# Placing the softmax rows of a transformer layer: a broadcast copy and a second transfer, or a short copy and one transfer

## The chip, the cores and the metric

The kernel runs on one core of a Trainium2 chip, as one launch. The metric is the device time of a run in microseconds. The kernel before took 1909.01, 1910.10 and 1910.19 us in three runs, with a median of 1910.1 us. The profiled execution is the first of them.

## The reference

A transformer block with 16 sequences of 256 positions and 512 features: self attention, cross attention to a context of 256 positions, and a feed-forward part of 2048 hidden features, each behind a layer norm whose gain and offset come from a conditioning vector.

```python
def _attn(q, k, v):                                   # 16 heads of 32 features
    scores = jnp.einsum('bqhd,bkhd->bhqk', q, k) * scale
    w = jax.nn.softmax(scores, axis=-1)
    return jnp.einsum('bhqk,bkhd->bqhd', w, v).reshape(B, L, D)

x = x + _attn(rope(xn1 @ Wq), rope(xn1 @ Wk), xn1 @ Wv) @ Wo        # xn1 = adaln(x, emb, ln1)
x = x + _attn(rope(xn2 @ Wq2), rope(ctx @ Wk2), ctx @ Wv2) @ Wo2    # xn2 = adaln(x, emb, ln2)
x = x + gelu(xn3 @ W1.T + b1) @ W2.T + b2                           # xn3 = adaln(x, emb, ln3)
```

## The kernel before

Every float32 product is made of three products of split operands (high by high, high by low, low by high). The kernel has two parts. The first, up to some 1210 us, does both attention layers: 32 items (16 sequences in each of two layers), each with 16 heads, so 512 heads in a row, in one order that all engines follow. The second part is the feed-forward, which the change does not touch.

The order is written out by `stage_order(B)`. It loops over the heads n and gives each head three places, 3n, 3n+1 and 3n+2. Place 3n begins with the score product of head n ("scores", line 619 on TensorE, the row maximum on VectorE at line 865, and exp with a row sum on ScalarE at line 750, step "total", at place 3n+2). Place 3n+1 begins with the second, transposed score product of head n-13 ("weigh", line 640; `LAG = 13`), whose exp on ScalarE (line 764) writes the probabilities that the "mix" step (line 655) takes. Projections, rotations, norms and loads are put at places between. Each engine has its own function (`attention_tensor`, `attention_scalar`, `attention_vector`, `attention_gpsimd`, `attention_sync`) that walks the same order and does its part of each step in that order, with semaphore waits; so a step that waits holds up all that stands behind it on its engine.

The change is about how the softmax shift enters the "weigh" product. Heads are handled in groups G of eight (64 groups; two per item; groups 0 to 31 are the first layer). For each group VectorE forms minus the row maximum minus the log of the row sum, split into a high and a low part: 16 numbers for each query ("max_split", lines 873 to 878, `max_parts`). TensorE transposes them ("max_turn", line 626), and they become rows 96 to 111 of `qT`, the moving operand of "weigh", below 96 rows of head data. `kT`, the stationary one, holds in its rows 96 to 111 a table of ones and zeros (`select`, written once by six ScalarE copies at the start) that picks, for each head, its high and its low row. `max_parts` is 112 columns wide with 96 columns of zeros, so that the transposed rows come out at partitions 96 to 111. There ScalarE copies them into `qT`, repeated four times for the four heads of a quad ("max_copy", line 732, 16 partitions by 1024 elements, semaphore `rows_placed`). A transfer from the SyncE queue copies the same rows to the second quad of the group ("max_again", line 1004, semaphore `rows_again`). The first weigh of a group waits for `rows_placed`, its fifth for `rows_again`.

The score-side results go through five PSUM banks in turn (`score_users`, `NS = 5`): "scores", "weigh", "max_turn" and "mix" each take the next bank, and TensorE waits (`scores_left`) until the user five before has been read.

## Time and profile before

| what | value |
|---|---|
| median of three runs | 1910.1 us |
| the profiled execution, its span | 1909.01 us, 1907.2 us |
| TensorE matmul busy | 1869.2 us, 98% |
| ScalarE, VectorE, GpSimd busy | 1434.9, 1289.4, 787.3 us |
| mean granted clock | 0.996 |
| line 732, the broadcast copies | 64, 65.3 us in all |
| line 1004, the second transfers | 64 of 64 KB, 3.0 us from issue to landing (median) |

The span is the time from the first to the last instruction; the run's time has some 1.8 us around it. A matmul's end is modelled in the profile, so TensorE at 98% can still hold short pauses; they show as gaps between the starts. PE is TensorE's matmul, PEld its weight load, ACT ScalarE, DVE VectorE, POOL GpSimd, and a q behind a name (SPq, ACTq) marks an instruction that the engine's sequencer runs, such as the issue of a transfer.

### The profile page before, as it was taken

How to read it: one execution, taken by the hardware profiler on the slowest of the kernel's cores; microseconds unless marked ns; L12 is line 12 of the kernel's file. 1: busy time of each engine (PE TensorE's matmuls, PEld its weight loads, DVE VectorE, ACT ScalarE, POOL GpSimd, SP SyncE). 2: the span in 40 equal slices, each digit the busy share in tenths (PEclk: the TensorE clock that was granted, in tenths of full speed). 3: DMA queues.
4: the chain of work that ended last, by engine and by line, in shares of the span. 5: the costliest groups of instructions: out<-in, count | busy, mean ns of one | idle time of the engine just before them, and what ended most of it. 6: DMA issues, size and time to landing. Idle time of an engine off the chain costs nothing. (4 is left out here: it accounts for less than half of the span.)

```text
span 1907.2 us, 39347 instructions
## 1 busy us (share of the span) xinstructions
PE 1869.2 (98%) x13460; PEld 1632.0 (86%) x13460; DVE 1289.4 (68%) x2249; ACT 1434.9 (75%) x3819; POOL 787.3 (41%) x818
## 2 busy tenths in 40 slices
PE   8899999999998999999999998999999999999999
PEld 6888888888887988988988987688898998989898
DVE  6877667777766776776776777346766667666754
ACT  5888888888887898888888899655656566666654
POOL 3634334433433454454454441014535445453531
PEclk9999999999998999999999999999999999999999
DMA  7777767676686787677677687433131322323130
GB/s 230 206 210 211 219 196 202 195 209 179 194 233 179 210 237 224 190 223 215 194 222 219 192 230 196 130 111 117 61 111 56 111 78 89 100 70 109 45 100 34
DMA packets 307378, 311.51 MB, mean 163 GB/s; under 512 B 22000, under 2 KB 259952, under 8 KB 307184
## 3 DMA queue, kind: packets, MB, share of 16 engines
q1 hardware_dynamic: 306576, 308.67, 55.4%
q8 instruction: 111, 1.82, 0.4%
q14 instruction: 83, 0.68, 0.1%
q10 hardware_dynamic: 608, 0.34, 0.1%
HBM read 212.46 MB, written 92.27 MB: 160 GB/s over the span
## 5 line engine op out<-in xcount | busy, mean ns | idle before, releaser
L750 ACT ACTIVATE ps_s<-ps_s,neg_max 128x256 f32<-128x256 f32 x1024 | 461.6, 454 | 45.4 <-DVE neg_max L865 42.3
L865 DVE TENSOR_REDUCE neg_max<-ps_s 128x2 f32<-128x512 f32 x512 | 349.7, 687 | 210.1 <-PE ps_s L619 209.6
L764 ACT ACTIVATE prob<-ps_s 128x512 f32<-128x512 f32 x512 | 307.9, 602 | 98.7 <-PE ps_s L640 94.4
L619 PE MATMUL ps_s<-kT,qT 96*128 96x256 f32 x1024 | 218.6, 295 | 11.7 <-ACT ps_s L750 7.5
L935 POOL TENSOR_TENSOR rope_c<-rope_c,rope_s 128x256 f32<-128x256 f32 x128 | 98.6, 771 | 312.9 <-DVE rope_s L840 312.9
L619 PEld LDWEIGHTS ps_s<-kT,qT 96*128 96x128 f32 x1024 | 168.7, 190 | 59.5 <-ACT ps_s L750 24.5
L640 PE MATMUL ps_s<-qT,kT 112*128 112x256 f32 x1024 | 208.2, 285 | 9.9 <-ACT ps_s L750 9.3
L750 ACT ACTIVATION_READ_ACCUMULATOR ps_s<-ps_s,neg_max 128x1 f32 x1024 | 217.9, 213 | 0.0
L609 PE MATMUL ps_g<-xx_hi,w_hi 128*128 128x256 f32 x1024 | 208.0, 284 | 1.4 <-issue 1.4
L609 PE MATMUL ps_g<-xx_hi,w_lo 128*128 128x256 f32 x1024 | 205.6, 282 | 0.0
L609 PE MATMUL ps_g<-xx_lo,w_hi 128*128 128x256 f32 x1024 | 205.4, 282 | 0.0
L1306 PE MATMUL ps_y<-w_hi,h_hi 128*128 128x512 f32 x512 | 201.5, 394 | 1.2 <-DVE h_lo L1431 1.2
L1306 PE MATMUL ps_y<-w_lo,h_hi 128*128 128x512 f32 x512 | 200.6, 392 | 0.0
L1306 PE MATMUL ps_y<-w_hi,h_lo 128*128 128x512 f32 x512 | 199.3, 389 | 0.0
L640 PEld LDWEIGHTS ps_s<-qT,kT 112*128 112x128 f32 x1024 | 169.5, 190 | 31.3 <-ACT ps_s L750 12.1
L1431 DVE TENSOR_TENSOR h_lo<-h_sb,h_hi 128x512 fp32r<-128x512 f32 x128 | 111.5, 875 | 103.9 <-ACT h_hi L1329 102.6
L942 POOL TENSOR_TENSOR rot_lo<-rope_c,rot_hi 128x512 fp32r<-128x512 f32 x128 | 166.1, 1298 | 30.4 <-ACT rot_hi L726 28.6
L923 POOL TENSOR_TENSOR xx_lo<-xT,xx_hi 128x512 fp32r<-128x512 f32 x66 | 86.9, 1318 | 197.0 <-ACT xx_hi L712 196.8
L1290 PE MATMUL ps_h<-xf_hi,cw_hi 128*128 128x256 f32 x592 | 167.5, 283 | 0.0
L1290 PE MATMUL ps_h<-xf_lo,cw_hi 128*128 128x256 f32 x592 | 165.8, 280 | 0.0
L1290 PE MATMUL ps_h<-xf_hi,cw_lo 128*128 128x256 f32 x592 | 165.7, 280 | 0.0
L609 PEld LDWEIGHTS ps_g<-xx_hi,w_hi 128*128 128x128 f32 x1024 | 158.2, 190 | 2.6 <-issue 1.5
(155 smaller groups left out, 4708.4 us busy)
## 6 DMA issues: line engine op xcount, KB each, us to landing
kT<-k_turned SPq DMA_DIRECT2D x384, 128.0 KB, 3.2
qT<-q_turned SPq DMA_DIRECT2D x128, 256.0 KB, 4.0
f_raw<-in_w1T SPq DMA_DIRECT2D x124, 256.0 KB, 3.0
k_turned<-rot_hi SPq DMA_DIRECT2D x64, 256.0 KB, 3.2
k_turned<-rot_lo SPq DMA_DIRECT2D x64, 256.0 KB, 2.5
q_turned<-rot_hi SPq DMA_DIRECT2D x64, 256.0 KB, 3.8
q_turned<-rot_lo SPq DMA_DIRECT2D x64, 256.0 KB, 4.2
qT<-q_turned SPq DMA_DIRECT2D x128, 128.0 KB, 4.1
```

Of the source, the lines that this page charges most:

```text
L609: ins = eng.matmul(ps_g[:, b, s * L:(s + 1) * L], w[:, row, (T * s + t) * P:(T * s + t + 1) * P], a[:, c, :], start=c == 0 and j == 0 and ...
L619: ins = eng.matmul(ps_s[:, score_bank(step), t * L:(t + 1) * L], qT[0:ROWS, quad % NQ, j, t * P:(t + 1) * P], kT[0:ROWS, quad % NQ, j, :], ...
L640: ins = eng.matmul(ps_s[:, score_bank(step), t * L:(t + 1) * L], kT[:, quad % NQ, j, t * P:(t + 1) * P], qT[:, quad % NQ, j, :], start=Tru ...
L750: ins = eng.activation(scores[:, t * L:(t + 1) * L], scores[:, t * L:(t + 1) * L], ACT.Exp, bias=neg_max[G % 2][:, t, j:j + 1], accum_out= ...
L764: eng.activation(prob[:, n % NP, :, :].rearrange("p t l -> p (t l)"), ps_s[:, score_bank(step), :], ACT.Exp).then_inc(exp_done, 1)
L865: eng.tensor_reduce(neg_max[G % 2][:, :, j], ps_s[:, score_bank(step), :].rearrange("p (t l) -> p t l", l=L), AX.X, ALU.max, negate=True). ...
L923: eng.tensor_tensor(lo[:, ks, :], xT[:, ks, :], hi[:, ks, :].bitcast(F32), ALU.subtract).then_inc(x_low_done, 1)
L935: eng.tensor_tensor(rope_c[n % 2][:, 0, :], rope_c[n % 2][:, 0, :], rope_s[:, 0, :], ALU.subtract)
L942: eng.tensor_tensor(rot_lo[:, n % NT, :, :], rope_c[n % 2][:, :, :], rot_hi[:, n % NT, :, :].bitcast(F32), ALU.subtract).then_inc(rot_lo_d ...
L1290: ins = eng.matmul(ps_h[:, bank(p, n), 0:L], w[:, cols], x_[:, k, :], start=n in OPENS and k == 0 and j == 0, stop=k == 1 and j == 2, skip ...
L1306: ins = eng.matmul(ps_y[:, t, :], h[:, t * P:(t + 1) * P], w, start=c == 0 and j == 0, stop=c == FC - 1 and j == 2)
L1431: eng.tensor_tensor(h_lo[a % NH][:, :], h_sb[a % 2][:, :], h_hi[a % NH][:, :].bitcast(F32), ALU.subtract).then_inc(h_lo_done, 1)
```

## The change

The group's 16 rows are laid out as 2 partitions by 8 heads instead of 16 partitions repeated for 4 heads, so that one high and one low row stand in `qT` below each head's own data, and `kT` needs only ones there. The operand has 98 rows instead of 112. Per group: the transposes yield 16 rows; ScalarE copies 16 partitions by 256 elements into a staging buffer `max_rows`; and one transfer issued from ScalarE's queue ("max_rows") puts them into both quads. The transfer from SyncE's queue is gone, and the first weigh of a group now waits for the landing of the transfer (`max_rows_in`). The "max_turn" step stays at place 32 of the group in the first layer and moves to place 30 in the second; the copy follows one place later and the transfer two places later. The six copies of `select` on ScalarE and its load are gone; a memset on VectorE writes the ones near the start.

```diff
-        for n, kind in ((24, "log"), (25, "max_split"), (32, "max_turn"), (33, "max_copy"), (35, "max_again")):
+        turn = 32 if G < 2 * B else 30
+        for n, kind in ((24, "log"), (25, "max_split"), (turn, "max_turn"), (turn + 1, "max_copy"), (turn + 2, "max_rows")):
             put(24 * G + n, kind, G)
...
     yield ("warm", WARM_START)
+    yield ("ones",)
...
-    for slot in range(2):
-        yield ("select", slot)                        # and twice more, six in all
...
-    MROWS = ROWS + 2 * HG
+    MROWS = ROWS + 2
...
-            max_parts = sb("max_parts", [P, T, MROWS])
-            select = sb("select", [P, HG])
+            max_parts = sb("max_parts", [P, T, ROWS])
+            max_rows = [sb(f"max_rows{n}", [2 * HG, L], F32R) for n in range(2)]
...
-                return {"scores": total_done, "weigh": exp_done, "max_turn": rows_placed, "mix": o_lo_done}[old[0]], nth[old]
+                return {"scores": total_done, "weigh": exp_done, "max_turn": maxes_copied, "mix": o_lo_done}[old[0]], nth[old]
...
-                            ins = eng.transpose(ps_s[0:MROWS, score_bank(step), t * P:(t + 1) * P],
-                                                max_parts[:, t, :], ident[:, :])
+                            ins = eng.transpose(ps_s[0:2 * HG, score_bank(step), t * P:(t + 1) * P],
+                                                max_parts[:, t, 0:2 * HG], ident[:, :])
...
                         if n % HG == 0:
                             G = n // HG
-                            eng.wait_ge(rows_placed, G + 1)
-                        elif n % HG == OH:
-                            eng.wait_ge(rows_again[n // HG % 2], 16 * (n // HG // 2 + 1))
+                            eng.wait_ge(max_rows_in[G % 2], 16 * (G // 2 + 1))
...
                     elif kind == "max_copy":
                         G = step[1]
                         eng.wait_ge(max_turned, G + 1)
+                        if G >= 2:
+                            eng.wait_ge(max_rows_in[G % 2], 16 * (G // 2))
+                        eng.activation(max_rows[G % 2][:, :], ps_s[0:2 * HG, score_bank(("max_turn", G)), 0:L],
+                                       ACT.Copy).then_inc(maxes_copied, 1)
+                    elif kind == "max_rows":
+                        G = step[1]
+                        eng.wait_ge(maxes_copied, G + 1)
                         if G >= NQ // 2:
                             eng.wait_ge(weigh_done, HG * (G - NQ // 2 + 1))
-                        eng.activation(qT[ROWS:MROWS, 2 * G % NQ, :, :],
-                                       ps_s[ROWS:MROWS, score_bank(("max_turn", G)), 0:L].unsqueeze(1).broadcast_to([2 * HG, OH, L]),
-                                       ACT.Copy).then_inc(rows_placed, 1)
+                        first = 2 * G % NQ
+                        into = qT[ROWS:MROWS, first:first + 2, :, :]
+                        eng.dma_start(into.rearrange("p g h l -> p (g h) l").bitcast(F32),
+                                      max_rows[G % 2][:, :].bitcast(F32)).then_inc(max_rows_in[G % 2], 16)
...
+                    elif kind == "ones":
+                        eng.memset(kT[ROWS:MROWS, :, :, :].bitcast(F32), 1.0).then_inc(ones_set, 1)
...
-                    elif kind == "max_again":
-                        G = step[1]
-                        eng.wait_ge(rows_placed, G + 1)
-                        eng.dma_start(qT[ROWS:MROWS, (2 * G + 1) % NQ, :, :].bitcast(F32),
-                                      qT[ROWS:MROWS, 2 * G % NQ, :, :].bitcast(F32)).then_inc(rows_again[G % 2], 16)
```

How the instructions move, at two places. First ScalarE around the copy of group 13 (odd, first layer): "total" rows are the exp with sum, `prob` rows the exp of weigh, `rot_hi` a rotated half. Before:

```order
L750 ACTIVATE ps_s,total<-ps_s,neg_max 128x256 x2
L764 ACTIVATE prob<-ps_s 128x512
L750 ACTIVATE ps_s,total<-ps_s,neg_max 128x256 x2
L732 ACTIVATE qT<-ps_s 16x1024
L764 ACTIVATE prob<-ps_s 128x512
L726 ACTIVATE rot_hi<-rope_c 128x512
L750 ACTIVATE ps_s,total<-ps_s,neg_max 128x256 x2
L764 ACTIVATE prob<-ps_s 128x512
```

and the same place now:

```order
L744 ACTIVATE ps_s,total<-ps_s,neg_max 128x256 x2
L758 ACTIVATE prob<-ps_s 128x512
L744 ACTIVATE ps_s,total<-ps_s,neg_max 128x256 x2
L725 ACTIVATE max_rows<-ps_s 16x256
L758 ACTIVATE prob<-ps_s 128x512
L719 ACTIVATE rot_hi<-rope_c 128x512
L734 DMA qT<-max_rows 2x8x256
L744 ACTIVATE ps_s,total<-ps_s,neg_max 128x256 x2
L758 ACTIVATE prob<-ps_s 128x512
```

The copy keeps its place and is shorter; the transfer stands behind an exp and a rotation. In the even groups of the first layer it stands behind the exp alone. Second, ScalarE around the copy of group 40 (even, second layer). Before:

```order
L764 ACTIVATE prob<-ps_s 128x512
L750 ACTIVATE ps_s,total<-ps_s,neg_max 128x256 x2
L726 ACTIVATE rot_hi<-rope_c 128x512
L732 ACTIVATE qT<-ps_s 16x1024
L764 ACTIVATE prob<-ps_s 128x512
L750 ACTIVATE ps_s,total<-ps_s,neg_max 128x256 x2
```

and the same place now:

```order
L758 ACTIVATE prob<-ps_s 128x512
L725 ACTIVATE max_rows<-ps_s 16x256
L744 ACTIVATE ps_s,total<-ps_s,neg_max 128x256 x2
L719 ACTIVATE rot_hi<-rope_c 128x512
L734 DMA qT<-max_rows 2x8x256
L758 ACTIVATE prob<-ps_s 128x512
```

The copy has moved ahead of a pair of exps with sum, and the transfer takes the place of the old copy. In the odd groups of the second layer no rotation stands between.

## Rows read from the trace of the kernel before

**Rows 1.** Busy time by stretch: us, then each engine's busy us (instructions), clock, DMA.
```profile
100.00:550.00 450.00, 448.02 (x3553) 386.02 (x3552) 322.19 (x587) 377.58 (x1133) 177.75 (x186) 1.00 0.70 201
584.00:594.50 10.50, 7.05 (x43) 4.06 (x44) 5.06 (x8) 9.49 (x27) 4.38 (x4) 0.51 0.77 209
600.00:1125.00 525.00, 524.25 (x4156) 460.13 (x4155) 366.80 (x693) 457.33 (x1368) 243.61 (x248) 1.00 0.73 211
1125.00:1207.00 82.00, 73.89 (x572) 59.90 (x571) 55.31 (x111) 77.28 (x237) 18.93 (x19) 1.00 0.65 174
```

**Rows 2.** Groups: line engine op, shapes, count | busy us, mean ns | idle before, releasers.
```profile
L732 ACT ACTIVATE qT<-ps_s 16x1024 fp32r<-16x1024 f32 x64 | 65.3, 1020 | 1.9 <-PE ps_s L626 0.3
L1334 ACT ACTIVATE u_sb<-ps_h 128x256 f32<-128x256 f32 x168 | 64.4, 383 | 83.1 <-PE ps_h L1290 81.9
L619 PE MATMUL ps_s<-kT,qT 96*128 96x256 f32 x1024 | 218.6, 295 | 11.7 <-ACT ps_s L750 7.5 <-ACT qT L732 1.5 <-DMA qT<-q_turned 1.5
L640 PE MATMUL ps_s<-qT,kT 112*128 112x256 f32 x1024 | 208.2, 285 | 9.9 <-ACT ps_s L750 9.3 <-DVE o_lo L884 0.6
L626 PE MATMUL ps_s<-ident,max_parts 128*112 128x128 f32 x128 | 24.4, 272 | 0.0
L582 PE MATMUL ps_g<-ident,xn 128*128 128x128 f32 x272 | 40.8, 273 | 1.3 <-DVE rope_s L840 1.3
```

**Rows 3.** Timeline, all engines, group 13: start us, us, engine line operation.
```profile
304.01 1.02 ACT L732 ACTIVATE qT<-ps_s 16x1024 fp32r<-16x1024 f32 x1
...
304.91 0.54 SPq L1000 DMA_DIRECT2D q_turned<-rot_lo  x1
...
305.06 0.60 ACT L764 ACTIVATE prob<-ps_s 128x512 f32<-128x512 f32 x1
...
305.55 0.62 ACT L726 ACTIVATE rot_hi<-rope_c 128x512 fp32r<-128x512 f32 x1
...
307.22 0.31 PEld L640 LDWEIGHTS ps_s<-qT,kT 112*128 112x128 f32 x2
307.33 0.40 PE L640 MATMUL ps_s<-qT,kT 112*128 112x256 f32 x2
```

**Rows 4.** Line 1000, stretch 304 to 307: its one transfer's landing.
```profile
DMA to landing us min/median/max: 2.4/2.4/2.4
```

**Rows 5.** Line 1004, whole span: landing of its 64 transfers.
```profile
DMA to landing us min/median/max: 2.3/3.0/6.2
```

**Rows 6.** Timeline around the copy of group 16, first layer.
```profile
359.44 1.02 ACT L732 ACTIVATE qT<-ps_s 16x1024 fp32r<-16x1024 f32 x1
360.49 0.60 ACT L764 ACTIVATE prob<-ps_s 128x512 f32<-128x512 f32 x1
...
362.57 0.31 PEld L640 LDWEIGHTS ps_s<-qT,kT 112*128 112x128 f32 x2
```

**Rows 7.** Timeline around the copy of group 40, second layer.
```profile
807.82 0.60 ACT L764 ACTIVATE prob<-ps_s 128x512 f32<-128x512 f32 x1 [0.38 <-PE ps_s L640]
...
809.22 0.64 ACT L726 ACTIVATE rot_hi<-rope_c 128x512 fp32r<-128x512 f32 x1
...
812.51 0.31 PEld L640 LDWEIGHTS ps_s<-qT,kT 112*128 112x128 f32 x2
```

**Rows 8.** Line 1004, stretch 560 to 595 (groups 27 and 28): landing.
```profile
DMA to landing us min/median/max: 4.9/5.3/5.7
```

**Rows 9.** Timeline at 563 us: a weigh that waited.
```profile
563.73 0.50 PE L640 MATMUL ps_s<-qT,kT 112*128 112x256 f32 x2 [1.43 <-ACT ps_s L750]
```

**Rows 10.** Lines 740 and 777: durations min/median/max ns; first statistics on VectorE.
```profile
L740 ACT ACTIVATE kT<-select x6: 1032/1046/1057, 27.9 to 37.4; 16x1024 fp32r<-16x1024 f32 x6
...
L777 DVE MEMSET max_parts<- x1: 245/245/245, 0.9 to 0.9; 128x224 f32 x1
...
8.67 0.69 DVE L787 BATCH_NORM_STATS2 stats<-xn 128x6 f32<-128x512 f32 x1 [7.53 <-DMA xn<-in_x]
```

**Rows 11.** Page, part 3: the SyncE queue's packets, MB, share of 16 engines.
```profile
q1 hardware_dynamic: 306576, 308.67, 55.4%
```

More of the change, by code:

```diff
@@ L217, in stage_order @@
     yield from rotated("q", 0)
-    for slot in range(2, 4):
-        yield ("select", slot)
     yield ("stack", "k", 0)
@@ L225, in stage_order @@
     yield from rotated("k", 1)
-    for slot in range(4, 6):
-        yield ("select", slot)
     for c in range(2, KC):
@@ L419, in block_kernel @@
             mod_parts = [prob_row[:, 2 * KC * D:(2 * KC + 1) * D], w_raw[:, 0, :], w_raw[:, 0, :]]
-            small_in = {name: sem(f"{name}_in") for name in ("cond", "lnb", "ident", "cos", "sin", "select")}
+            small_in = {name: sem(f"{name}_in") for name in ("cond", "lnb", "ident", "cos", "sin")}
             x_in, res_in, ctx_in = (sem(n) for n in ("x_in", "res_in", "ctx_in"))
@@ L424, in block_kernel @@
             stack_in = {m: [sem(f"stack_{m}{n}") for n in range(4)] for m in "qk"}
-            rows_placed, rows_again = sem("rows_placed"), [sem(f"rows_again{n}") for n in range(2)]
+            max_rows_in = [sem(f"max_rows_in{n}") for n in range(2)]
             STACKS = {"q": 2, "k": 3}
@@ L433, in block_kernel @@
             mod_copied = sem("mod_copied")
-            w_hi_done, x_full, x_hi_done, ctx_hi_done, rot_hi_done, v_done, exp_done, total_done, log_done, o_hi_done = (
+            w_hi_done, x_full, x_hi_done, ctx_hi_done, rot_hi_done, v_done, maxes_copied, exp_done, total_done, log_done, o_hi_done = (
                 sem(n) for n in ("w_hi_done", "x_full", "x_hi_done", "ctx_hi_done", "rot_hi_done", "v_done",
-                                 "exp_done", "total_done", "log_done", "o_hi_done"))
+                                 "maxes_copied", "exp_done", "total_done", "log_done", "o_hi_done"))
             parts_cleared = sem("parts_cleared")
@@ L440, in block_kernel @@
             early_done, early_kept = sem("early_done"), sem("early_kept")
-            constants_set, select_set, mod_summed, mod_added, norm_stats, norm_means, norm_var, x_normed, x_low_done, ctx_low_done = (
-                sem(n) for n in ("constants_set", "select_set", "mod_summed", "mod_added", "norm_stats", "norm_means", "norm_var",
+            constants_set, ones_set, mod_summed, mod_added, norm_stats, norm_means, norm_var, x_normed, x_low_done, ctx_low_done = (
+                sem(n) for n in ("constants_set", "ones_set", "mod_summed", "mod_added", "norm_stats", "norm_means", "norm_var",
                                  "x_normed", "x_low_done", "ctx_low_done"))
@@ L662, in attention_scalar @@
                 eng.dma_start(ident[:, :], ident_in).then_inc(small_in["ident"], 16)
-                eng.dma_start(select[ROWS:MROWS, :], pick).then_inc(small_in["select"], 16)
                 eng.dma_start(ln_b[:, :, :], lnb).then_inc(small_in["lnb"], 16)
@@ L729, in attention_scalar @@
                         eng.wait_ge(max_turned, G + 1)
+                        if G >= 2:
[5 more added lines that the diff above has]
+                        eng.wait_ge(maxes_copied, G + 1)
                         if G >= NQ // 2:
                             eng.wait_ge(weigh_done, HG * (G - NQ // 2 + 1))
-                        eng.activation(qT[ROWS:MROWS, 2 * G % NQ, :, :],
-                                       ps_s[ROWS:MROWS, score_bank(("max_turn", G)), 0:L].unsqueeze(1).broadcast_to([2 * HG, OH, L]),
-                                       ACT.Copy).then_inc(rows_placed, 1)
-                    elif kind == "select":
-                        slot = step[1]
-                        if slot == 0:
-                            eng.wait_ge(small_in["select"], 16)
-                        first = slot % 2 * OH
-                        eng.activation(kT[ROWS:MROWS, slot, :, :], select[ROWS:MROWS, first:first + OH].unsqueeze(2).broadcast_to([2 * HG, OH, L]),
-                                       ACT.Copy).then_inc(select_set, 1)
+                        first = 2 * G % NQ
+                        into = qT[ROWS:MROWS, first:first + 2, :, :]
+                        eng.dma_start(into.rearrange("p g h l -> p (g h) l").bitcast(F32),
+                                      max_rows[G % 2][:, :].bitcast(F32)).then_inc(max_rows_in[G % 2], 16)
                     elif kind == "total":
@@ L776, in attention_vector @@
             def attention_vector(eng):
-                eng.memset(max_parts[:, :, :], 0.0).then_inc(parts_cleared, 1)
+                eng.memset(max_parts[:, :, 0:ROWS], 0.0).then_inc(parts_cleared, 1)
                 eng.memset(neg_half[:, :], -0.5).then_inc(constants_set, 1)
```

6 lines of the change are left out of this document (3 added, 3 removed).

## The prediction

> **What bounds the kernel now.** I read the busy times by stretch first. In the steady part of both attention layers TensorE is busy 448.02 of 450 us and 524.25 of 525 us, at the full granted clock of 1.00, while ScalarE, the next, is busy 84% and 87% [rows 1]. So the reader should see a TensorE that hardly ever waits there: time taken off ScalarE gives nothing back in these 975 us, and any new wait of TensorE is paid in full. Only the last stretch of the second layer, 1125 to 1207 us, is different: TensorE 73.89 of 82 us, ScalarE 77.28 of 82, which is 94% [rows 1]. Of the weigh products' waits over the whole span, 9.3 us were for the exps of line 750 [rows 2]. Smaller stretches of that kind are the first groups and the change of layer, where a piece of 10.5 us ran at a granted clock of 0.51, TensorE's lower level (1.2 GHz) [rows 1]. Over the whole span the two score products stood idle 11.7 and 9.9 us [rows 2]; that is about all that a lighter ScalarE could ever buy.
>
> **The copy.** It shrinks from 1020 ns to about 383 ns, the mean of another ScalarE copy of 256 elements out of PSUM [rows 2]. That is 0.64 us for each of 64 groups, 41 us of ScalarE's time. In the steady part TensorE covers all of it: value 0. In the ScalarE-bound stretch there are six groups (58 to 63), so at most 6 x 0.64 = 3.8 us. But ScalarE's queue also gets the transfer's issue, which holds a sequencer for 0.54 us [rows 3]. If it lies beside a running exp it costs nothing, if not it eats nearly the whole gain: between 0 and 3.8 us, and I take a gain of 1.5, since in these groups the issue stands behind the short read of the row sum, which can't cover it.
>
> **The transfer in front of weigh.** This is the term that matters. Before, the first weigh waited for a ScalarE copy that was long done. Now it waits for a chain: copy, the exp behind it, in odd groups a rotation too, issue, landing. Queued behind a waiting weigh on TensorE is everything, and all other engines live off that.
>
> Odd groups of the first layer. The copy starts at 304.01 and would end at 304.39; the exp, which followed the old copy by 0.03 us, starts at 304.42. The rotation followed that exp by 0.49 us, so 304.91; it had not waited for its input. The issue comes with it, about 304.95. The weight load of the first weigh stood at 307.22 [rows 3]: 2.27 us are left. A transfer that SyncE issued at 304.91, the same moment, took 2.4 us to land [rows 4]; the old row transfers never took less than 2.3 [rows 5]. I take 2.4 to 2.5: it lands at 307.4, 0.2 us late. A product that had to wait also starts worse, as a pair takes 0.50 us instead of 0.40 [rows 3, 9], so 0.3 us a group. There are 14 such groups (3 to 29): 4.2 us.
>
> Even groups of the first layer. The tighter kind, group 16 and eight others like it: copy 359.44 to 359.82, exp at 359.85, issue at 359.90; the weight load is at 362.57, so 2.67 us are left [rows 6], more than 2.5. Cost 0, but with 0.2 us to spare. The rest have some 0.4 us more.
>
> Second layer. The copy now follows the exp at 807.82 by 0.50 us: 808.32 to 808.70, then the pair of exps with sum (0.90 us, from 808.32 to the rotation at 809.22), the rotation at 809.63, the issue at 809.67, and 2.84 us are left until 812.51 [rows 7]. Cost 0. The odd groups have no rotation in between and more room. The exps with sum finish 0.4 us later than before there; the bank they free is needed only by the score product of two heads later, so this is covered.
>
> Groups 0, 1, 27 and 28 stand where the DMA engines are crowded. The row transfers there took 4.9 to 5.7 us [rows 8], against 2.3 to 2.8 us of room: 2 us or more late each at worst, nothing at best if the transfer, now alone in its own queue, overtakes. As ScalarE bounds there and has work in stock while TensorE waits, part is hidden. I take 2 us in all (0 to 8).
>
> **The rest.** Weigh has 98 rows instead of 112: 96-row and 112-row products took 295 and 285 ns, so fewer rows buy nothing [rows 2]; 0. The transposes of 112 and of 128 columns took 272 and 273 ns [rows 2], so 16 columns change nothing I can see; 0, at most 128 x 0.03 = 4 us if a short weight load counts for once. The six select copies (6 x 1.046 us) lie between 27.9 and 38.5 us [rows 10], where ScalarE otherwise waits for rotations; 0.1 us gained. The memset of 2 x 6144 elements, at 245 ns for 224 elements, is 6.7 us and ends at 7.8; VectorE's next work began at 8.67, when its input had landed [rows 10]. Covered by that load; uncovered it would cost up to 6.7. SyncE loses 64 issues of some 0.6 us and their waits, and nothing there is late in the steady part: 0.
>
> **Sum.** 4.2 + 2.0 - 1.5 - 0.1 = +4.6 us on the profiled execution's 1909.01 us, which is 1913.6. That execution lies 1.1 us below the median of its three runs, so I forecast 1914 us, against 1910.1. What a measurement of this kernel can tell from no change is 0.2%, or 3.8 us, so this lies on the edge.
>
> **Rival 1, eight rows in a line (slower).** The target is only two partitions. If the 16 KB don't spread over all DMA engines but go as eight 1 KB packets one behind the other, each of 55 ns (0.554 x 16 x 1907.2 us / 306576 packets) [rows 11], landing comes 0.4 us later, and 0.8 if each alternates with SyncE's. With a landing of 2.8: odd groups 0.53 + 0.1 late, x 14 = 8.8; nine tight even groups 0.13 + 0.1, 2.1; second layer 0. With 2.5 for the rest, 1920 to 1922. With 3.3 it reaches 16 + 7 + 1, plus the second layer's even groups at 0.56 x 13 = 7, 1940. It decides once landing exceeds about 2.7 us.
> The Trainium skill has a rule that speaks for this rival: "DMA: Bandwidth & Descriptors", section "Why a DMA increments its semaphore by 16 and not by 1", says that a hardware-issued transfer is spread over the largest number up to 16 that divides the slowest dimension on both sides, which for 2 rows of target is two engines. No row of before shows which engines a transfer used. By that rule the sum would be some 1921, by the row of line 1000 alone 1914.
>
> **Rival 2, ScalarE's time comes back (faster).** Ten groups lie where ScalarE bounds: 10 x 0.64 = 6.4 us if the issues are hidden beside exps, and if TensorE's pause before 584 us shrinks, the piece at half clock goes too, worth up to half of its 10.5 us, 5. That needs rows that land in time: 1898 to 1903. For it speaks the 94% [rows 1], against it that all waits of the two score products come to 21.6 us, first stretches included [rows 2], and that the transfer adds its own latency.
>
> **Rival 3, all hidden.** Landing takes 2.3 us and the crowded groups overtake: 1908 to 1911.
>
> **Chances.** Forecast 0.35, rival 1 0.20, rival 2 0.20, rival 3 0.25. All of rival 2 is faster: 0.20. No change is rival 3 and a third of the forecast: 0.37. Slower is the rest, 0.43. The range leaves out the low end of rival 2 and the far end of rival 1: 1902 to 1925; the forecast's own is 1910 to 1919.
>
> **What would show it.** Right: weigh (640 before) waits for "DMA qT<-max_rows" in some 14 groups of the first layer, 0.1 to 0.3 us each, and none in the second; the new transfer lands in 2.4 to 2.5 us; ScalarE some 41 us less busy; the stretch 1125 to 1207 about 1.5 us shorter. Wrong: waits for that transfer in even groups as well, or a landing over 2.7 us (rival 1); no wait at all (rival 3); a granted clock that stays at 1.00 near 584 us (rival 2); VectorE's first statistics after 8.7 us.

## The result, and the profile after

The changed kernel took 1929.57 us (median of four runs, 1926.05 to 1929.88) against 1910.14 for the kernel before; the ratio is 1.0095, with an interval of 1.0078 to 1.0112. It is slower, and outside the predicted range of 1902 to 1925. The profiled execution took 1925.28 us, with a span of 1923.5 us; that is 16.3 us more than the 1909.01 us of before.

Busy time by stretch in the changed kernel, with the columns of [rows 1]; the last row is a second of the places where TensorE ran at its lower level:

```profile
100.00:550.00 450.00, 440.63 (x3461) 377.72 (x3460) 314.76 (x572) 354.74 (x1110) 172.86 (x180) 1.00 0.66 196
600.00:1125.00 525.00, 521.50 (x4119) 456.65 (x4120) 366.80 (x692) 435.89 (x1372) 244.04 (x248) 0.99 0.72 210
577.80:581.20 3.40, 3.40 (x31) 1.66 (x24) 0.21 (x1) 2.44 (x7) 0.00 (x0) 0.51 1.04 340
```

Against [rows 1] TensorE has lost 7.4 us of work in the 450 us of the first layer, and ScalarE has 22.8 us less to do there. Most of the loss is in the first layer and at its ends; the rest is in the last groups. The groups of the page and of the view by line that answer to [rows 2]:

```profile
L725 ACT ACTIVATE max_rows<-ps_s 16x256 fp32r<-16x256 f32 x64 | 22.8, 357 | 0.0
L615 PE MATMUL ps_s<-kT,qT 96*128 96x256 f32 x1024 | 216.5, 293 | 10.7 <-ACT ps_s L744 8.3 <-DVE o_lo L880 1.0 <-DMA qT<-q_turned 0.7
L634 PE MATMUL ps_s<-qT,kT 98*128 98x256 f32 x1024 | 211.6, 289 | 24.4 <-DMA qT<-max_rows 21.8 <-ACT ps_s L744 1.9 <-DVE o_lo L880 0.6
L622 PE MATMUL ps_s<-ident,max_parts 128*16 128x128 f32 x128 | 24.4, 271 | 2.2 <-ACT ps_s L744 2.2
L622 PEld LDWEIGHTS ps_s<-ident,max_parts 128*16 128x16 f32 x128 | 11.0, 88 | 6.9 <-ACT ps_s L744 2.8 <-ACT prob L758 0.3
```

Weigh (line 634 now) waits 21.8 us for the new transfer, where [rows 2] has no such entry at all. The waits, by group, from TensorE's idle time before the first weigh: none in any odd group from 3 to 29; in the even groups 2, 6, 8, 12, 18, 20 and 26 of the first layer 2.4, 1.8, 1.2, 1.1, 0.6, 0.2 and 1.5 us (8.9 together, where the expectation of number 1 below has 9.1); in groups 1, 27, 28, 30, 59, 60 and 62 1.7, 2.3, 2.8, 0.4, 1.3, 4.0 and 0.5 us (13.0 together).

The semaphores' events in the trace give the landing of each of the 64 transfers: 2.2 us at the least, 2.29 in the median, 6.2 at the most. Each transfer raises its semaphore three times, about 1.1 us after the issue and twice at the end. In a quiet group its sixteen 1 KB packets go in pairs, eight steps in 0.45 us; in group 6 they go as two runs of eight, one starting 0.5 us behind the other.

Group 13, the place of [rows 3]; timeline of ScalarE's engine and queue, start us, us, engine line operation:

```profile
313.63 0.36 ACT L725 ACTIVATE max_rows<-ps_s 16x256 fp32r<-16x256 f32 x1
...
313.90 0.57 ACT L758 ACTIVATE prob<-ps_s 128x512 f32<-128x512 f32 x1
...
314.02 0.62 ACTq L734 DMA_DIRECT2D qT<-max_rows  x1
...
314.38 0.62 ACT L719 ACTIVATE rot_hi<-rope_c 128x512 fp32r<-128x512 f32 x1
```

The issue starts 0.03 us after the copy's end (313.99), while the exp runs, and ahead of the rotation that stands in front of it in the order. The weight load of the group's first weigh stands at 316.91 and its product at 317.02: there are 2.9 us of room, not 2.27, and the landing takes 2.25. In the even groups of the first layer the issue does not come so early: in group 16 the exp in front of it waits 0.37 us for its weigh product, and the issue starts 0.44 us after the copy's end, with 2.47 us left until the weight load.

Now two even groups of the first layer, 6 and 16, with the same order on ScalarE: first the timeline from the residual load of SyncE to the first weigh, then the stretches of 1 us from the issue on (last two columns: DMA share, GB/s).

```profile
175.82 0.43 SPq L1022 DMA_DIRECT2D res<-in_x  x1
...
176.30 0.47 SPq L968 DMA_DIRECT2D w_raw<-in_lnT  x1
...
178.04 0.65 ACTq L734 DMA_DIRECT2D qT<-max_rows  x1
...
182.58 0.47 PE L634 MATMUL ps_s<-qT,kT 98*128 98x256 f32 x2 [1.80 <-DMA qT<-max_rows]
```

```profile
366.97 0.43 SPq L1022 DMA_DIRECT2D res<-in_x  x1
...
369.66 0.62 ACTq L734 DMA_DIRECT2D qT<-max_rows  x1
...
372.24 0.40 PE L634 MATMUL ps_s<-qT,kT 98*128 98x256 f32 x2
```

```profile
178.04:179.04 1.00, 1.00 (x11) 1.00 (x10) 1.00 (x3) 0.84 (x2) 0.00 (x0) 1.00 1.12 243
179.04:180.04 1.00, 1.00 (x11) 1.00 (x10) 1.00 (x2) 1.00 (x5) 0.87 (x2) 1.00 1.03 324
180.04:181.04 1.00, 0.74 (x7) 0.54 (x5) 0.40 (x2) 0.98 (x4) 0.57 (x1) 1.00 1.10 397
...
369.66:370.66 1.00, 1.00 (x11) 1.00 (x10) 1.00 (x3) 0.87 (x2) 0.00 (x0) 1.00 0.98 348
370.66:371.66 1.00, 1.00 (x11) 1.00 (x10) 1.00 (x2) 1.00 (x5) 0.87 (x2) 1.00 0.15 45
```

In group 16 the DMA engines run empty 1 us after the issue; the first packet of the rows starts 1.27 us after it and they land in 2.24. In group 6 the engines are full for 3 us; the first packet starts after 3.0 us, the landing takes 4.41, and TensorE stands still for 1.80 us. In these two groups the 16 KB are in time only where SyncE's earlier transfers, 512 KB of residual above all, have drained.

Why does the residual load stand there at all? In the kernel before SyncE waited for the copy of the rows, to issue the second transfer, and the residual load stood behind that. Group 16 before, timeline of SyncE (the copy is the one of [rows 6], at 359.44):

```profile
360.50 0.57 SPq L1004 DMA_DIRECT2D qT<-qT  x1
361.11 0.58 SPq L1031 DMA_DIRECT2D res<-in_x  x1
```

The load came 1.67 us after the copy's start. The change took SyncE's wait away, and now the load is issued 2.69 us ahead of the rows (366.97 and 369.66 above). The same happened in group 60, where TensorE waits longest:

```profile
1174.52 0.43 SPq L1022 DMA_DIRECT2D res<-x_after_self  x1
```

The rows of group 60 are issued at 1175.77, 1.25 us behind it, and land after 6.2 us; the row transfer of before was issued there 0.63 us ahead of the residual load and landed in 2.35. So the 21.8 us of waits are of two kinds. In groups 6, 18, 20, 26 and 60, together 8.1 us, the old row transfer had landed in 2.3 to 2.4 us, and the load that came forward makes the new one late. In groups 1, 2, 8, 12, 27, 28, 30 and 59, together 13.2 us, the old one had already taken 3.0 to 6.2 us, unseen since its user came half a group later. Group 62 waits 0.5 us with a landing of 2.26: its place is too near.

**The sum.** Against the profile of before: waits for the rows +21.8; weigh's waits for the exps with sum from 9.3 to 1.9, so -7.4; the scores' idle time from 11.7 to 10.7, -1.0; the transposes' 0 to 2.2, +2.2; three pieces of 3.4 us at a granted clock of 0.50 that begin near the end of long waits (106.7, 577.7 and 1181.9 us) and that before did not have, half of 10.2, +5.1; and the transposes' weight load, 88 ns for 16 columns against 132 for 112, 128 x 0.044, -5.6. That is +15.1 of the 16.3. The waits are read off; the clock's term is an estimate, half of the time spent at the lower level; that the shorter load pays is argued, from its size and from the second layer: from group 32 to 57, without waits, the changed kernel gains 0.1 us a group on the one before.

### The profile page after: what moved, and what is told of

The parts are those of the page before. It is cut to its first block and busy times, and to the rows that moved or that the text cites. A ratio compares the mean times of both kernels' runs of the same rounds, so it can differ in the third digit from the quotient of the medians.

```text
span 1923.5 us, 39339 instructions
## 1 busy us (share of the span) xinstructions
PE 1869.4 (97%) x13460; PEld 1630.4 (85%) x13460; DVE 1294.9 (67%) x2250; ACT 1383.3 (72%) x3813; POOL 785.8 (41%) x818
## 5 line engine op out<-in xcount | busy, mean ns | idle before, releaser
L744 ACT ACTIVATE ps_s<-ps_s,neg_max 128x256 f32<-128x256 f32 x1024 | 452.8, 443 | 55.4 <-DVE neg_max L861 48.3
L758 ACT ACTIVATE prob<-ps_s 128x512 f32<-128x512 f32 x512 | 303.4, 593 | 137.2 <-PE ps_s L634 134.3
L634 PE MATMUL ps_s<-qT,kT 98*128 98x256 f32 x1024 | 211.6, 289 | 24.4 <-DMA qT<-max_rows 21.8
L615 PE MATMUL ps_s<-kT,qT 96*128 96x256 f32 x1024 | 216.5, 293 | 10.7 <-ACT ps_s L744 8.3
L634 PEld LDWEIGHTS ps_s<-qT,kT 98*128 98x128 f32 x1024 | 169.3, 191 | 46.9 <-issue 21.0
L744 ACT ACTIVATION_READ_ACCUMULATOR ps_s<-ps_s,neg_max 128x1 f32 x1024 | 207.8, 203 | 0.0
```

The costliest lines, as they stand in the source:

```text
L615: ins = eng.matmul(ps_s[:, score_bank(step), t * L:(t + 1) * L], qT[0:ROWS, quad % NQ, j, t * P:(t + 1) * P], kT[0:ROWS, quad % NQ, j, :], ...
L634: ins = eng.matmul(ps_s[:, score_bank(step), t * L:(t + 1) * L], kT[:, quad % NQ, j, t * P:(t + 1) * P], qT[:, quad % NQ, j, :], start=Tru ...
L744: ins = eng.activation(scores[:, t * L:(t + 1) * L], scores[:, t * L:(t + 1) * L], ACT.Exp, bias=neg_max[G % 2][:, t, j:j + 1], accum_out= ...
L758: eng.activation(prob[:, n % NP, :, :].rearrange("p t l -> p (t l)"), ps_s[:, score_bank(step), :], ACT.Exp).then_inc(exp_done, 1)
```

## The experiments

Twelve kernels, in three sittings; each ratio is to the kernel before, run on the same chip beside it. Unless said otherwise the edit is made to the changed kernel. Theory A is the latency: room of 2.6 to 3.0 us, and a landing that is 2.24 us plus whatever SyncE has put in front.

**1. The residual load seven places later.**

```diff
-            put(p + 37, "res_load", i - 1)
+            put(p + 44, "res_load", i - 1)
```

> The change, with one number altered: the step that loads the residual (512 KB on SyncE's queue) stands at place 44 of an item instead of 37, so behind the rows' transfer and its landing. Theory (collision): in the kernel before SyncE's queue itself waited for the row copy (line 1004) and so held the residual load back; now it is issued up to 2.7 us before the rows' transfer and fills the DMA engines while that is to land. Then the waits of weigh for the rows in the even groups of the first layer (9.1 us in the changed kernel) fall to 3 us or less, and the time falls by 5 to 9 us against the change, to about 1921 to 1924. Rival (few rings): the transfer is slow because its target is two partitions; then it lands late as before and the time stays at 1929. Groups 1, 27, 28, 59 and 60 are crowded for other reasons and stay.

Measured: 1933.92 us, ratio 1.0134 (1.0097 to 1.0170); waits for the rows 22.2 us, 16 times. A miss: I had expected 5 to 9 us less than the changed kernel, and it is no faster. The even groups 16 to 26 now landed in 2.23 to 2.29 us and did not wait, as A says, but groups 2, 6, 8, 10 and 12 still did, and the load now met the rows of odd groups 11, 15, 19, 25 and 31. The collision was moved, not removed.

**2. SyncE held back until the copy is done.**

```diff
+ (35, "hold"): on SyncE, eng.wait_ge(maxes_copied, G + 1)
```

> The change, and SyncE's queue waits at place 35 of each group until ScalarE has made the copy, as in the kernel before, but issues nothing there. Theory (collision): nothing that stands behind place 35 can be ahead of the rows' transfer any more; residual, weight and context loads and the stacks behind it come after. Waits for the rows fall from 21.8 us to 8 to 12 us (what is left is groups 1, 27, 28, 59 and 60, where the crowd is issued before the copy), and the time by 7 to 12 us against the change, to 1918 to 1922. Rival (few rings): no change, 1929.

Measured: 1942.17 us, ratio 1.0164 (1.0138 to 1.0190); waits 33.8 us, 19 times: a miss in sign. All even groups from 2 to 26 waited. Group 16, timeline:

```profile
379.16 0.40 SPq L1024 DMA_DIRECT2D res<-in_x  x1
...
379.57 0.62 ACTq L734 DMA_DIRECT2D qT<-max_rows  x1
```

SyncE is released by the same copy and issues its 512 KB 0.41 us ahead of ScalarE; the rows' first packet then starts 2.62 us after the issue in place of 1.27 (2.6 to 3.1 in groups 16 to 24), and they land after 3.89 us. To hold the other queue until the copy isn't enough: the load must stand behind the rows.

**3. The transposes at place 30 in both layers.**

```diff
-        turn = 32 if G < 2 * B else 30
+        turn = 30
```

> The change, with the transposes of a group at place 30 in the first layer too (32 in the change). This gives the chain copy, transfer, weigh two places more, some 1.5 us. Theory (collision): the late landings of 0.3 to 1.8 us in the first layer's even groups are covered but for the longest; waits fall by 6 to 9 us in the first layer, time about 1920 to 1923. The transposes may now wait for the split of the maxima, at most 0.5 us in a few groups. Rival (the latency isn't what costs, but ScalarE's queue with the issue in it): the time stays at 1929.

Measured: 1916.53 us, ratio 1.0027 (1.0016 to 1.0039). 13 us came back by nothing but room. Weigh and transposes:

```profile
L634 PE MATMUL ps_s<-qT,kT 98*128 98x256 f32 x1024 | 213.8, 291 | 13.3 <-DMA qT<-max_rows 9.5 <-ACT ps_s L744 3.2 <-DVE o_lo L880 0.6
L622 PE MATMUL ps_s<-ident,max_parts 128*16 128x128 f32 x128 | 24.4, 271 | 9.4 <-DVE max_parts L874 6.8 <-ACT ps_s L744 2.6
```

The waits for the rows fell from 21.8 to 9.5 us, though the landings in even groups did not get shorter (2.3 to 5.4 us). Of the new waits of the transposes for VectorE's split, 0.5 us in each of 14 odd groups, little reaches the time: over those groups the distance to the kernel before grows by 0.1 us each.

**4. The kernel before, its second transfer issued from ScalarE's queue.**

```diff
-  "max_again" in attention_sync
+  "max_again" in attention_scalar, same place
```

> The kernel before, with one part moved: the second transfer (qT to qT, line 1004) is issued from ScalarE's queue at the same place 35, so SyncE's queue no longer waits for the copy. Theory (collision): the residual load goes out earlier here too and the second transfer lands later in the even groups, but the fifth weigh has some 9 us for it, so nothing waits: within 0.1% of the kernel before, 1909 to 1912. Rival (freeing SyncE's queue disturbs the rest, for instance the stacks): slower by 3 us or more. Rival (an issue in ScalarE's queue costs 0.5 us each): slower in the stretch that ScalarE bounds, by up to 3 us.

Measured: 1910.74 us, ratio 0.9998 (0.9988 to 1.0007). Issues on ScalarE and a freer SyncE cost nothing where the transfer has half a group of slack.

But the landings change, and nothing else was moved in this kernel. Group 60, landing of the second transfer, first in the kernel before (line 1004, stretch 1163 to 1165), then here (line 738, stretch 1165.3 to 1165.5):

```profile
DMA to landing us min/median/max: 2.3/2.3/2.3
DMA to landing us min/median/max: 8.9/8.9/8.9
```

In groups 6, 18, 20 and 26 the landing was 2.3 to 2.4 us and is now 5.5, 4.0, 2.6 and 4.6; in groups 14, 16 and 22, where the residual load goes out 3.1 to 4.3 us ahead, it stays at 2.3. The residual load is now issued ahead of the transfer (in group 60 at 1162.70, the transfer at 1165.39). So it is the freed SyncE queue that makes these groups late, whatever the rows' layout; the change put a transfer that TensorE waits for into that place.

**5. A small residual load.** From the second sequence of the first layer on, the load brings 8 of 128 partitions.

```diff
-                        eng.dma_start(res[:, :, :], ...
+                        few = P if layer or i == 0 else 8
+                        eng.dma_start(res[0:few, :, :], ...
```

> In the first layer the residual load of SyncE (line 1022, 512 KB) brings only 8 of 128 partitions (32 KB), from the second batch on; the residual of those batches is therefore wrong, all else is the changed kernel. Nothing else moves. Theory A (the rows of maxima are late in even groups because the residual load, issued 2.2 to 2.7 us ahead from the other queue, is in front of them on the DMA engines): the waits of weigh in groups 6, 8, 12, 18, 20, 24, 26 (8.4 us together) go to under 1 us, group 2 (whose load stays whole) keeps its 2.5 us, as do 27, 28, 59, 60; sum of weigh's waits for max_rows 21.8 to about 13.5 us, time about 1921 us (1918 to 1924) against 1929.6 for the changed kernel. Rival (a transfer into two partitions on a queue of its own is slow now and then, whatever SyncE loads): waits stay near 22 us and the time near 1929.

Measured: 1924.59 us, ratio 1.0060 (1.0045 to 1.0074). Half a hit. In the even groups 14 to 24 every transfer landed in 2.24 to 2.46 us and none waited; group 18 went from 0.6 us to 0, group 20 from 0.2 to 0, group 26 from 1.5 to 0.4. That is 2 us of waits; in all the profiled execution, at 1933.70 us the slowest of the four, still waited 21.5 us for rows, 12 times, where I had expected 13.5. Groups 6, 8, 10 and 12 waited 1.5, 1.3, 1.8 and 1.7 us, together more than in the changed kernel, and groups 2, 28 and 59 3.2, 4.6 and 2.6. In groups 6 to 12 the rows' issue follows 1.6 to 2.7 us behind weight loads of 256 KB and, in 8, 10 and 12, 0.6 to 1.3 us behind a stack of `kT`, which the theory should have counted: what is in front is all of SyncE's queue, and the residual is the largest piece only from group 14 on.

**6. Rows of even groups from SyncE, ahead of the residual load; odd ones from ScalarE.**

```diff
 attention_scalar, "max_rows":   + if G % 2 == 0: continue
 attention_sync,   "max_rows":   + the same step, if G % 2: continue
```

> The rows of maxima of even groups are issued by SyncE at the place where the row transfer of before stood, directly ahead of the residual load; those of odd groups stay on ScalarE. Theory A (what counts is who stands in front on the DMA engines: in SyncE's own queue the residual load is generated after the rows): even groups 2 to 26 land in 2.3 to 2.6 us and wait no more than in before (0 to 1 us in all), left are groups 1, 27, 28, 59, 60 with perhaps 8 us; time 1917 us (1912 to 1922). Rival (what counts is the chain copy, issue, landing by itself): SyncE adds a wait for the copy and the issue comes no earlier, so even groups stay late: 1928 or more. A third way: the wait for the copy holds back SyncE's stack loads, and the products wait for kT or qT instead, which would show as a wait for k_turned or q_turned.

Measured: 1997.56 us, ratio 1.0448 (1.0430 to 1.0466): 80 us off my number, and both halves of it teach. The waits for the rows make 69.2 us, 24 times, and the very first weigh stands still for 6.4 us more. Group 16, timeline, and the wait of group 8 behind it:

```profile
388.63 0.36 ACT L725 ACTIVATE max_rows<-ps_s 16x256 fp32r<-16x256 f32 x1
...
389.02 0.68 SPq L1008 DMA_DIRECT2D qT<-max_rows  x1
...
389.74 0.40 SPq L1035 DMA_DIRECT2D res<-in_x  x1
...
392.01 0.40 PE L634 MATMUL ps_s<-qT,kT 98*128 98x256 f32 x2
```

```profile
220.20 0.36 ACT L725 ACTIVATE max_rows<-ps_s 16x256 fp32r<-16x256 f32 x1
...
222.76 0.60 SPq L1022 DMA_DIRECT2D qT<-q_turned  x1
223.41 0.43 SPq L970 DMA_DIRECT2D w_raw<-in_lnT  x1
223.93 0.70 SPq L1008 DMA_DIRECT2D qT<-max_rows  x1
...
228.15 0.47 PE L634 MATMUL ps_s<-qT,kT 98*128 98x256 f32 x2 [3.98 <-DMA qT<-max_rows]
```

Where SyncE is already waiting for the copy (groups 4, 6 and 14 to 26) the rows are issued 0.02 to 0.03 us behind it and land in 2.29 to 2.30 us (group 6: 2.85), with 512 KB right behind them; not one of these groups waits. This is what A says of the order in the queue. Where SyncE is still busy with what stands ahead in its own program (groups 8, 10, 12, and the even ones from 28 to 58) the issue comes 2.8 to 4.6 us after the copy's end, and weigh waits 2.0 to 9.0 us. The third way that I had named, waits for `qT` or `kT` in their place, hardly came (2.0 us, once).

**7. One head more between scores and weigh.**

```diff
-LAG = 13
+LAG = 14
```

> The changed kernel with weigh (and mix) following the scores by 14 heads instead of 13: one head more, some 2.27 us, lies between the copy and the first weigh of a group. Theory A (a latency that varies from 2.2 to 6 us against 2.6 to 3.0 us of room): with 4.9 to 5.3 us of room only groups 60 and perhaps 59 still wait, 1 to 2 us together; the extra half clock pieces go; the one head more costs about 1 to 2 us once at the end of the weighing; time 1913 us (1909 to 1918). Rival (the loss is TensorE's own: the transposes, the products of 98 rows or the clock): the time stays near 1929. Second rival (later weighing keeps the tiles of rotated q longer and makes SyncE's stack loads late): waits for q_turned in their place.

Measured: 1925.20 us, ratio 1.0063 (1.0050 to 1.0075); the profiled span is 1918.8.

```profile
PE ps_s L615 <- ACT ps_s L744: 10.9, 23, 2.1
PE ps_s L634 <- ACT ps_s L744: 5.8, 9, 1.6
PE ps_s L634 <- DMA qT<-max_rows: 3.6, 4, 1.7
```

(The columns are the us in total, the times, the longest.) The time is a miss, 12 us above my number; the waits for the rows are not far off, 3.6 us in 4 groups where I had expected 1 to 2, with landings of up to 6.9 us: they are hidden by room. The price was under-estimated: the other order lets the scores and weigh wait for ScalarE (10.9 and 5.8 us, against 8.3 and 1.9), and the distance to the kernel before grows by some 0.2 us a group in the first layer, where the changed kernel's fell by 0.1 between its waits. The sum of waits predicts the profiled span, not all of the median.

**8. The kernel before, transposes at 30 in its second layer.**

```diff
-        for n, kind in (..., (32, "max_turn"), (33, "max_copy"), (35, "max_again")):
+        turn = 32 if G < 2 * B else 30
+        for n, kind in (..., (turn, "max_turn"), (turn + 1, "max_copy"), (35, "max_again")):
```

> The kernel before, with only the other edit of the change's order: in the second layer the transposes and the copy of the maxima stand two places earlier (30 and 31 in place of 32 and 33), the copy still to all four heads. If the fall of 0.1 us a group that the changed kernel showed in its second layer comes from this move, the second layer gets 2.5 to 3 us shorter: 1907.5 us; if it comes from the lighter work of ScalarE or the 98 rows, the time is that of before within 1 us. I expect no change: 1910 (1908 to 1912).

Measured: 1923.75 us, ratio 1.0057 (1.0045 to 1.0069). A miss: not the same but slower.

```profile
PE ps_s L620 <- ACT ps_s L751: 16.2, 34, 2.2
```

(Us in total, times, the longest.) The scores wait 16.2 us for ScalarE against 7.5 before [rows 2], some 0.5 us in every second group from 38 on. Not all of it is the edit's: 3.6 us of the distance stand before the second layer, where nothing was moved, 6.5 us come between groups 37 and 59, and most of the rest behind them. With the long copy the earlier place doesn't fit; with the short one (the changed kernel) it costs nothing. So ScalarE's relief has a value after all: it pays for the move that the transfer needs (as number 11 shows).

**9. The place by parity.**

```diff
+        turn = 28 if G in (28, 60) else 32 if G < 2 * B and G % 2 else 30
```

> The changed kernel with max_turn at place 30 in even groups of the first layer (room to the first weigh 4.1 us in place of 2.6) and at 32 in odd ones (3.0 us, and no wait of the transposes for the split of VectorE, which cost 0.5 us in each odd group with 30 everywhere), and at 28 in groups 28 and 60. Theory A, summed from the run with 30 everywhere (1916.5): minus 14 x 0.5 for the transposes, minus about 2 for groups 28 and 60: 1908 us (1905 to 1913), with waits for max_rows of 6 us or less. Rival (what is gained in rows is paid again by the scores, whose bank ScalarE frees later, as in the kernel before with turn 30): 1915 or more.

Measured: 1923.41 us, ratio 1.0054 (1.0039 to 1.0068); waits for rows 14.7 us, 10 times. My sum was wrong by 15 us. Up to group 28 the run is level with number 3 (10.6 and 10.8 us behind before), so the 7 us that I had taken for the transposes' waits were not there to be had. The rest is lost between groups 28 and 29 (+4.3, where number 3 gains 1.4), beside the place 28; group 60's landing was 6.6 us and made nothing of its head start.

**10. The same with the residual load at 44.** The two edits of 9 and 1 together.

> The same with the residual load seven places later (44). Theory A: with even groups' rows now 1.5 us earlier, the later load is clear of them altogether, but it meets the odd groups' rows, which have only 3.0 us, as it did in the first run of this study (groups 11, 15, 19, 25, 31): no better than the run beside it, 1911 us (1906 to 1918). Rival (the load's place does not matter once even groups have 4.1 us): equal within 1 us.

Measured: 1934.77 us, ratio 1.0123 (1.0102 to 1.0144), waits 16.0 us: worse than beside it. Odd groups 11, 15, 19 and 31 waited again, 0.8 to 2.4 us, and group 27 for 5.5 us. The rows of the odd groups are late as written, the time is a miss: the median lies 17 us above the top of my range, and the waits for rows are only 1.3 us more than in number 9. The profiled execution, 1928.62 us, is the fastest of five; where the other four lost up to 12.6 us more is not shown.

**11. The transposes at place 32 in the second layer too.**

```diff
+        turn = 32
```

> The changed kernel with max_turn at 32 in the second layer too, as the kernel before had it. The room of its even groups shrinks from 3.7 to some 2.2 us, against a landing of 2.25 to 2.3: theory A expects a wait of 0.1 to 0.4 us in 13 even groups, some 3 to 5 us, and odd groups (5.4 to some 3.9 us of room, landing 2.3 to 4.1) late by little: 1935 us (1931 to 1940). Rival (the second layer's order is no matter): 1929.

Measured: 1941.24 us, ratio 1.0153 (1.0139 to 1.0167); waits for rows 32.8 us, 27 times. The dose in the other direction: from the issue to the first weigh there were 2.6 us in place of 3.7 in the even groups of the second layer, and 3.1 in place of 5.4 in the odd ones, and that cost some 11 us. A's sign and mechanism, at twice its size: all the even groups from 32 to 58 waited, 0.1 to 1.6 us, and four odd ones 0.1 to 1.1. Issued later, the rows met other loads and landed in 2.6 to 3.9 us in all of these even groups but one.

**12. Two transfers of one target partition each.**

```diff
-  one dma_start, max_rows (16 rows) into qT[ROWS:MROWS, two quads]
+  for r in range(2): dma_start, eight rows into qT[ROWS + r:ROWS + r + 1, two quads]
```

> The changed kernel with the rows moved by two transfers of one target partition each, on ScalarE's queue. The records of the changed kernel show the sixteen 1 KB packets in pairs, eight steps of 0.05 us. If a transfer uses as many DMA engines as divide its target's partitions, each of the two uses one, the second issue comes 0.6 us later and the landing with it: floor 2.24 becomes about 2.9 us. Then odd groups (3.0 us) are just in time, even groups (2.6 us) late by 0.4 to 0.5 us in every one, 14 x 0.45 = 6 us more: 1935 us (1931 to 1940). Rival (few engines are what makes the rows slow in crowded groups, and two transfers spread over more): the long landings shorten and the time falls below 1929.

Measured: 1947.99 us, ratio 1.0196 (1.0179 to 1.0212). Group 16, timeline:

```profile
379.16 1.32 ACTq L735 DMA_DIRECT2D qT<-max_rows  x2
...
381.91 0.48 PE L634 MATMUL ps_s<-qT,kT 98*128 98x256 f32 x2
```

Right in sign, low in size, and wrong in the step: the semaphore's record has eight events of data for each transfer, not one, and eight small packets behind the data, where the one of two partitions and sixteen rows had two of each. I read that as eight engines and two. In quiet groups the first transfer lands after 1.95 us in place of 2.24, and the second, issued 0.6 us later, after 2.61 in even groups and 3.3 in odd ones (why so late there stays open), so that weigh starts 2.75 and 3.45 us behind the first issue, where 2.6 and 3.0 were the room. 25 waits make 28.2 us. In the crowded groups four times the engines help nothing: group 6 lands after 4.9 us (4.4 with two), group 60 after 6.35 (6.2). So the number of engines is worth some 0.3 us in a quiet group and is not what makes the rows late in a crowded one.

No version beat the kernel before. Number 3 is the nearest, 5 us behind it. Not tried were its combination with SyncE's queue for the even groups 4, 6 and 14 to 26 alone, where it waits 4 of its 9.5 us at the most, and a single transfer spread over eight engines.

## Why the prediction was wrong

**What bounds.** Right. TensorE had no slack in both layers, and each wait of weigh came out as time: +12.4 us up to the start of group 28, and +5.3 for groups 59 and 60.

**The copy.** 357 ns measured for 383; ScalarE is 51.6 us less busy (1434.9 to 1383.3), of which the copies are 42.5. Its value in the steady part was put at nothing. In the trace weigh's waits for ScalarE fell by 7.4 us, which I had bounded at 3.8 for the last groups; number 8 shows the same relief from the other side. Part of that may only be hidden behind the waits for rows: in numbers 7 and 9, with 3.6 and 14.7 us of these, it is 5.8 and 6.4 us again. In the stretch where I expected -1.5 us, groups 59 and 60 lost 5.3 to the landing. (The sum itself was rounded down: 4.6 us on the median of 1910.1 is 1914.7, not 1914.)

**Odd groups, +4.2.** Wrong. I queued the issue behind the start of the rotation, because the rotation stands in front in the order. The issue ran beside the exp, 0.4 us before the rotation began. 0.6 us more of room (2.9 for 2.27), and no odd group from 3 to 29 waited: 0.

**Even groups, 0, and SyncE, 0.** This is the step that failed. Room and quiet landing were near: 2.67 us predicted to the weight load, 2.47 in group 16, because the exp in front of the issue waited 0.37 us for its weigh product, which the long copy had hidden; 2.4 and 2.24 us for the landing. But seven of 13 even groups waited, 8.9 us. I had put the freeing of SyncE at nothing, since nothing there was late. It was early that counted: in the kernel before SyncE's wait for the copy held the residual load back behind the row transfer, and the change let it out 2.2 to 2.7 us ahead of the new one in groups 6, 18, 20 and 26. Number 4 shows this by itself, in the kernel before; number 5, with the load small, and number 6, with the rows ahead of it in the same queue, show the way back: the even groups 14 to 24 land in 2.2 to 2.5 us in both (group 26, with a context load in front in number 5, in 3.0 there and in 2.3 in number 6). With group 60 it comes to 8.1 us. Groups 2, 8 and 12, 4.7 us, are another matter: I took one landing from one row [rows 4] for all groups, and left the spread of [rows 5], 2.3 to 6.2 us with a median of 3.0, to the groups that I already called crowded. In 2, 8 and 12 the old transfer took 4.2 to 5.4 us; it was covered by half a group of slack, so this never showed in TensorE's waits.

**Second layer, 0.** Right up to group 58, with more to spare than I wrote: 3.56 us in group 40 for 2.84, by the same misreading as in the odd groups, since the issue ran beside the exps with sum.

**Groups 0, 1, 27, 28, +2.** The place was right and the size was not: groups 1, 27 and 28 waited 6.9 us, and 30, 59, 60 and 62, which I had left out, 6.1 us. Room alone brings part of this back (numbers 3 and 7); which load stands in front in each of these groups was tested only for group 60, in number 4. The hope that a transfer in a queue of its own overtakes is refuted by number 2 and by group 60 (6.2 us). I had named 5.7 us of landing against 2.3 of room and then chosen near the kind end.

**Clock.** Not in the sum at all. Near the end of the waits of groups 2, 27 and 60 (2.3 to 4.0 us) a piece of 3.4 us at the lower level began (0.50 granted, 1.2 GHz), by my estimate 1.7 us lost each time. The stretch of 10.5 us in [rows 1] came back as one of 10.2 us at 598 us.

**The transposes, 0, at most 4.** A gain of up to 5.6 us, from the load of 16 columns; argued, not isolated.

**The memset.** It took 5.2 us for the 6.7 that I had estimated and ended at 7.6. VectorE's first statistics began at 9.05 us, after the 8.7 that I had named as a sign of being wrong, but what they waited for was again their input.

**The rivals.** Rival 2's relief was in part real, but was more than eaten. Rival 1 came nearest in time (1920 to 1940) and was right that the landing decides; its cause was not. The packets do go as two runs, in pairs when it is quiet, which fits what the rule that I quoted says of two target partitions (the Trainium skill, "DMA: Bandwidth & Descriptors", section "Why a DMA increments its semaphore by 16 and not by 1"; the semaphore's three events fit it too). But eight steps take 0.45 us and the quiet landing was 2.24 with them, under the 2.7 from which the rival decides, and number 12, where by that rule and by the events eight engines serve each transfer, is no better in a crowded group. The rule that bore on this case is one that I did not weigh: the same page, "Issuing engines are not separate DMA queues", says that transfers end up on the same 16 engines and interleave, whoever issued them. The trace agrees, and number 2 gives the price: a first packet that starts 2.6 to 3.1 us after the issue, in place of 1.27, behind a load issued 0.41 us earlier.

## What to carry to other kernels

When a change takes a wait out of a queue, look at what stood behind that wait. It comes forward, and here it came forward into the way of the one transfer that the bounding engine had begun to wait for. When a change puts a small transfer on the path of the bounding engine, compare its room with the landings at each place, not with one row, and list what the other queues will issue in the 3 us ahead of it in the new order. The old landings alone don't tell: in groups 6, 18, 20, 26 and 60 they were 2.3 to 2.4 us and the new ones 2.8 to 6.2, and in the odd groups from 3 to 25 they were 3.1 to 4.8 and the new ones 2.2 to 2.3. Time saved on a second engine is worth what it lets you move, so the move and the saving have to be judged together.

## What was unexpected of the hardware

- An issue on ScalarE's queue (0.62 us) began 0.03 us after the copy that it waited for, beside the exp, and ahead of the start of the rotation that stands in front of it in the program (group 13). It did not pass an exp that was still waiting for its product: in group 16 the exp started at 369.60 us and the issue at 369.66.
- The queue of its own gave no priority: in the quiet groups 3, 13 and 16 the first packet started 1.3 us after the issue; with 512 KB issued 0.41 us earlier from the other queue (number 2, groups 16 to 24), 2.6 to 3.1 us after; issued from SyncE's queue just ahead of the same 512 KB, the rows landed in 2.3 us.
- The stops of TensorE of 2.3 to 4.0 us (groups 2, 27 and 60; that of group 28 lay in the longer piece at 598 us) went with 3.4 us at the lower clock level, and those of 1.7 and 1.8 us (groups 1 and 6) did not, in this trace. This is no limit: in number 3 the stop of 1.7 us in group 6 was followed by such a piece, at 180.7 us.
- A transfer to two partitions ended in two data events of its semaphore, one to a single partition with eight heads in eight; in quiet groups they landed in 2.24 and 1.95 us.
